# The window mask of a local attention layer: written into PSUM by VectorE instead of by two TensorE products, with the value projection moved ahead of the scores

## What is computed

```python
q, k, v = split(shift_tokens(x) @ Wqkv)            # 16 heads of 64
q = rotary(l2norm(q) * qs);  k = rotary(l2norm(k) * ksc)
# windows of 32 queries, each against its own 32 keys and the 32 before them
mask = (it < jb) | (it > jb + w) | (jb == -1)
sim = einsum('bhwie,bhwje->bhwij', bq, bk2) * 8.0
sim = where(mask, -finfo.max, sim)
out = einsum('bhwij,bhwje->bhwie', softmax(sim), bv2)
x = out @ Wo + x
```

## Time and profile before

| | us |
|---|---|
| median of 3 runs | 2062.97 (2062.51 to 2063.5) |
| the profiled execution | 2057.26 |
| its span in the profile | 2055.5 |
| PE busy | 1935.8 (94%) |
| DVE busy | 1512.3 (74%) |
| ACT busy | 1299.4 (63%) |
| POOL busy | 1012.4 (49%) |

### The profile page before, as it was taken

How to read it: one execution, slowest core, us unless ns; L and a number is a source line. 1 busy time by engine, 2 the same in 40 slices (tenths; PEclk the granted TensorE clock), 3 DMA queues, 4 the chain that set the end, 5 groups by cost and what they waited for, 6 DMA issues and landing times.

```text
span 2055.5 us, 46953 instructions
## 1 busy us (share of the span) xinstructions
PE 1935.8 (94%) x19084; PEld 1159.1 (56%) x19084; DVE 1512.3 (74%) x1720; ACT 1299.4 (63%) x1840; POOL 1012.4 (49%) x727
## 2 busy tenths in 40 slices
PE   6798887899999999999999999999999999999996
PEld 3121134466666666666666666666666666666662
DVE  4898355687777777787778777877787778777862
ACT  3387834566666666666667666766676667666752
POOL 6200133575556555555555555555555555555530
PEclk9799999899999999999999999999999999999998
DMA  4231010343434443344434434443354334443430
GB/s 126 46 75 29 8 39 9 104 132 101 108 88 113 124 128 90 98 103 129 122 96 112 104 101 122 123 104 91 101 139 119 95 88 112 114 110 83 117 93 16
DMA packets 105541, 195.87 MB, mean 95 GB/s; under 512 B 14288, under 2 KB 34256, under 8 KB 105072
## 3 DMA queue, kind: packets, MB, share of 16 engines
q1 hardware_dynamic: 105328, 192.88, 36.2%
HBM read 124.81 MB, written 54.79 MB: 87 GB/s over the span
## 4 chain that ended last, share of the span: by engine, by line
PE 78%; ACT 2%; issue 1%; POOL 1%; DVE 0%; DMA 0%; SPq 0%; ACTq 0%; POOLq 0%
PE ps L1392 16%; PE ps L1467 9%; PE ps L1422 9%; PE ps L1444 8%; PE ps L1401 8%; PE ps L1477 8%; PE ps L1496 6%; PE ps L1455 4%; PE ps L1432 4%; PE ps L1506 3%; PE ps L1417 2%; ACT l_v_tok L1558 1%; PE ps L1484 1%; POOL l_rot L1365 0%; POOL l_rot L1368 0%
## 5 line engine op out<-in xcount | busy, mean ns | idle before, releaser
L1365 POOL TENSOR_TENSOR l_rot<-l_rot,l_rot_s 128x1024 f32<-128x1024 f32 x192 | 455.1, 2371 | 1.0 <-DVE l_rot_s L1709 1.0
L1354 POOL COPY l_kb<-l_kb 128x512 f32<-128x512 f32 x95 | 63.1, 664 | 683.5 <-ACT l_kb L1592 683.5
L1368 POOL TENSOR_TENSOR l_rot<-l_rot,l_norms 128x1024 f32<-128x1024 f32 x192 | 365.1, 1902 | 15.0
L1697 DVE TENSOR_TENSOR l_rot<-ps,l_tab_c 128x1024 f32<-128x1024 f32 x192 | 234.9, 1224 | 165.5 <-ACT l_sq L1566 165.5
L1566 ACT ACTIVATE l_sq<-ps 128x1024 f32<-128x1024 f32 x192 | 196.8, 1025 | 206.5 <-PE ps L1392 204.0
L1709 DVE TENSOR_TENSOR l_rot_s<-ps,l_tab_s 128x512 f32<-128x512 f32 x384 | 245.6, 682 | 0.0
L1688 DVE TENSOR_REDUCE l_norms<-l_sq 128x16 f32<-128x1024 f32 x192 | 232.1, 1209 | 0.0
L1392 PE MATMUL ps<-l_wqkv,xsT 128*128 128x512 f32 x384 | 187.1, 611 | 16.9 <-ACT l_v_tok L1558 14.4
L1592 ACT ACTIVATE l_kb<-ps 64x1024 f32<-64x1024 f32 x192 | 195.7, 1019 | 1.3
L1575 ACT ACTIVATE l_norms<-l_norms 128x16 f32<-128x16 f32 x192 | 41.6, 217 | 233.0 <-POOL l_norms L1362 233.0
L1444 PE MATMUL ps<-l_vb,l_pT 128*32 128x128 f32 x6144 | 186.9, 273 | 1.6 <-ACT l_pT L1558 1.4
(11 more groups left out here) (171 smaller groups left out, 3132.3 us busy)
## 6 DMA issues: line engine op xcount, KB each, us to landing
l_vb<-v_scratch SPq DMA_DIRECT2D x336, 256.0 KB, 4.5
v_scratch<-l_v_tok SPq DMA_DIRECT2D x96, 512.0 KB, 4.8
l_vb<-v_scratch SPq DMA_DIRECT2D x48, 192.0 KB, 3.2
xsT<-xT SPq DMA_DIRECT2D x48, 135.8 KB, 2.5
l_xf<-xT SPq DMA_DIRECT2D x48, 128.0 KB, 2.3
stack<-scratch SPq DMA_DIRECT2D x72, 64.0 KB
l_wqkv_odd<-wqkv SPq DMA_DIRECT2D x9, 512.0 KB, 6.7
scratch<-parts SPq DMA_DIRECT2D x12, 256.0 KB, 2.8
```

The source lines that it names most:

```text
L1365: nc.gpsimd.tensor_tensor(rot[:, t % 2, n], rot[:, t % 2, n], rot_s[:, n], ALU.add).then_inc(added, 1)
L1368: nc.gpsimd.tensor_tensor(rot[:, t % 2, n], rot[:, t % 2, n], norms[:, t % 2, n, :, None].broadcast_to([P, HEADS, DH]), ALU.mult).then_inc ...
L1697: nc.vector.tensor_tensor(rot[:, t % 2, 1 - r], slot(name, t).rearrange("p n (h d) -> p (n h) d", d=DH), tab_c[:, 1 - r, t % TILES, None, ...
```

## The change

- `scores` loses its two mask products. A new VectorE function `lay_mask(t-1)` copies the fp32 mask of the tile's kind from the constants into the slot of the scores, 128 x 1024 elements, and counts `mask_laid`. It waits until the transposed k, which stood in that slot, has been copied out. It stands on VectorE between the sine part of k (in the hidden step: the scaled feed-forward input) and the cosine part of q. TensorE's scores wait for `mask_laid` in place of the transposed k's release.
- The transposes of q and k set `start` only on the first of the four in a bank, where `nc.tensor.transpose` set it on each.
- `project_v(t)` moves ahead of `scores(t-1)` on TensorE, and its turn in slot 1 stays behind the mean.
- `copy_v(t)` on ScalarE moves from behind `inverse_norm(t, 1)` to directly behind `inverse_norm(t, 0)`.
- The constants hold one [128, 2 x 64] fp32 mask in place of the [128, 512] one and the selection matrix; the two casts at the start of the layers go away.

```diff
-        mask = sb("l_mask", [P, BANK], BF16)
-        mask_sel = sb("l_mask_sel", [P, 2, P], BF16)
+        mask = const("wmask").rearrange("p (a k) -> p a k", a=2)
...
+            if has(t):
+                plan(("v", t), 1)
             if has(t - 1):
                 plan(("s", t - 1), 3)
             if has(t - 2):
                 plan(("o", t - 2), 0)
-            if has(t):
-                plan(("v", t), 1)
...
-                        m = nc.tensor.transpose(dst[:, c // 4, (c % 4) * P:(c % 4 + 1) * P],
-                                                rot[:, t % 2, "qk".index(name), 2 * c:2 * c + 2, :], ident)
+                        m = nc.tensor.matmul(dst[:, c // 4, (c % 4) * P:(c % 4 + 1) * P],
+                                             rot[:, t % 2, "qk".index(name), 2 * c:2 * c + 2, :], ident,
+                                             is_transpose=True, start=(c % 4 == 0), stop=True, skip_group_check=True)
...
                     wait_free(pe, "qT", t)
-                    wait_free(pe, "kT", t)
+                    wait(pe, mask_laid, t + 1)
                     wait(pe, carried, t)
-                    if t == 0:
-                        pe.wait_ge(consts_set, 3)
                     take(pe, "s", t)
                     dst = slot("s", t)
-                    opening = int(t % TILES == 0)
-                    for n in range(2):
-                        rows = slice(64 * n, 64 * n + 64)
-                        nc.tensor.matmul(dst[:, n, :], mask_sel[rows, opening, :], mask[rows, :], start=True, stop=False,
-                                         skip_group_check=True)
...
+                    if has(t):
+                        project_v(t)
                     if has(t - 1):
                         scores(t - 1)
                     if has(t - 2):
                         values(t - 2)
-                    if has(t):
-                        project_v(t)
...
                     if has(t):
                         inverse_norm(t, 0)
+                        copy_v(t)
...
                     if has(t):
                         inverse_norm(t, 1)
-                    if has(t):
-                        copy_v(t)
...
-                nc.vector.tensor_copy(mask[:, :], const("wmask")).then_inc(consts_set, 1)
-                nc.vector.tensor_copy(mask_sel[:, :, :], const("wsel").rearrange("p (a q) -> p a q", a=2))\
-                    .then_inc(consts_set, 1)
...
+                def lay_mask(t):
+
+                    wait_free(dve, "kT", t)
+                    nc.vector.tensor_copy(slot("s", t).rearrange("p n (h k) -> p (n h) k", k=2 * WINDOW),
+                                          mask[:, int(t % TILES == 0), None, :].broadcast_to([P, HEADS, 2 * WINDOW]))\
+                        .then_inc(mask_laid, 1)
+
...
                         nc.vector.tensor_tensor(xg[:, :], cen[:, :], rstd[:, :], ALU.mult).then_inc(xn_ready, 1)
+                    if has(t - 1):
+                        lay_mask(t - 1)
                     if has(t):
                         cosine_part(t, 1)
                         sum_squares(t, 1)
```

More of the change, by code:

```diff
@@ L44 @@
                   ("kmask", HEADS), ("vmask", GROUPS * HEADS), ("ropeC", 2 * TILES * DH),
-                  ("ropeS", 2 * TILES * DH), ("wmask", 8 * 2 * WINDOW), ("wsel", 2 * P)):
+                  ("ropeS", 2 * TILES * DH), ("wmask", 2 * 2 * WINDOW)):
     CONST[_name] = (_at, _n)
@@ L1148, in layers @@
         slot_free = [sem(f"l_slot{i}_free") for i in range(4)]
+        mask_laid = sem("l_mask_laid")
         maxed, exped, sum_ready, inv_ready = (sem("l_" + n) for n in ("maxed", "exped", "sum_ready", "inv_ready"))
@@ L1573, in inverse_norm @@
                     if part == 0:
-                        act.wait_ge(consts_set, 3)
+                        act.wait_ge(consts_set, 1)
                     nc.scalar.activation(norms[:, t % 2, 1 - r], norms[:, t % 2, 1 - r], ACT.Ln, scale=65536.0)\
@@ L1850, in shape_constants @@
         put(name, a.reshape(2, TILES, P, DH).transpose(2, 0, 1, 3))
-    m = np.zeros((P, 8, 2 * WINDOW))
+    m = np.zeros((P, 2, 2 * WINDOW))
     key = np.arange(2 * WINDOW)
-    for r in range(WINDOW):
+    for q in range(P):
+        r = q % WINDOW
         bad = (key < r) | (key > r + WINDOW)
-        m[r] = np.where(bad, -1e30, 0.0)
-        m[WINDOW + r] = np.where(bad | (key < WINDOW), -1e30, 0.0)
-    m[2 * WINDOW:] = m[:2 * WINDOW]
+        m[q, 0] = np.where(bad, -1e30, 0.0)
+        m[q, 1] = np.where(bad | ((key < WINDOW) & (q < WINDOW)), -1e30, 0.0)
     put("wmask", m)
[L1860 to L1865, removed]
     return c
```

## The result

The changed kernel takes 2128.87 us (median of 4 runs, 2125.66 to 2142.47) against 2062.74 us before: a ratio of 1.0306, 95% interval 1.0265 to 1.0348. It is 66 us slower; the forecast was 59 us slower, 2122 us, with a range of 2084 to 2155.

The account below looks back on a forecast made before the run. TensorE's own work was taken to bound the kernel. Norm-step cycles +32, clock loss +30, early steps -4 and drain +1 made +59 us on 2063, so 2122 us; range 2084 to 2155.

Parts of the forecast that it names:

- What bounds the kernel: Layers: TensorE's own instructions set the time almost throughout; work removed there saves its length, a wait added costs its length.
- The gain forecast for the last step: Last of the four successive steps: 15.05 us, that is -0.58, as small waits go with the mask products.
- The mask copy: VectorE, every step: 1.2 us, ending near k+7.9 in former idle time, hidden because TensorE reaches the scores at k+8.8.
- The lower value, 0.85 us: Mask copy on VectorE: some 0.85 us for 1024 elements, from the 512-element cast; the sum would be some 10 us smaller.
- the hold-up to 2.3 us: Rival: the mask copy is held up like the second cast, to 2.3 us; 2182 us in all, chance 0.05.
- The norm step: v waits in slot 1 for the centring, TensorE idle 3.1 us; 17.26 us against 15.08, +2.18.
- The hidden step: The second feed-forward product waits some 0.5 us for slot 3, freed near k+14.7: 18.1 us, +0.1.
- The clock: Behind the norm step's idle time TensorE's clock halves, three times in four, costing 1.7 us each: +30 us.
- The early steps: Steps 1 to 5: k's wait for v's copy goes, VectorE sets a pace near 13.7 us; -0.6 each, -4 in all.
- The rival without the clock loss: Norm step: the same idle time but the clock is held, +29, 2092 us; chance 0.18.
- The rival in which v isn't held: Norm step: the centring frees the slot before TensorE gets there, step 14.19 us; 2020 us in all, chance 0.08.
- Break-even: Norm step: without a clock loss the change costs nothing if the centring ends near k+9.4; each microsecond earlier gives back one.

Follow-up runs that it names:

- the mask copy alone: The change without its new order, v and its copy where they were before: 2125.95 us, ratio 1.0322 to the kernel before.
- the experiment with the other bank first: The change, but in the norm step v's product for slot 1's second bank goes ahead of the wait for the centring: 2095.75 us, ratio 1.0139.
- the new order alone: The kernel before with the change's order of v and its copy, the mask still by two TensorE products: 2140.96 us, ratio 1.0376.
- the experiment with other work in the idle time: The change plus three unused 128x512 products between mean and v in each norm step: 2100.8 us, ratio 1.0186 to the kernel before.
- the norm step in its old order: The change, but in the norm step v goes behind scores and values again, its copy behind q's inverse norm: 2036.13 us, ratio 0.987.

## Why the prediction was right

**What bounds the kernel.** Right. In the output step TensorE is busy 19.34 of 19.34 us, and 0.32 us came off exactly as the mask products went. Last step 15.08 us against 15.05 worked out. Counting what every step does once, in the step without waits, and adding each step's own piece and its wait gave all four step lengths within 0.15 us. The gain forecast for the last step, 0.58 us, was too large all the same: it was taken from the one last step in the earlier trace rows, which took 15.63 us, while the median before was 15.47. Measured are 0.39.

**The mask copy.** Right in size, 1226 ns for 1.2 us, and in place. The lower value, 0.85 us from the cast of 512 elements, is excluded, and so is the hold-up to 2.3 us: the 96 copies of the program took 1217 to 1229 ns, 95 of them with GpSimd busy for over 97% of their length. What had held up the second cast in the earlier trace rows may be read from the trace before: it ran until 359.59, and a GpSimd product that had begun ahead of it until 359.44. By the Trainium skill's page "VectorE: DVE Perf Modes", section "Why PSUM operands drop a tier", an fp32 instruction of VectorE with an operand in PSUM goes no faster than the plain rate. The trace agrees: the copy takes as long as VectorE's products of 1024 elements that read PSUM, 1.22 to 1.23 us. That v covers the copy was the forecast's other half; the mask copy alone showed what it costs without v in front, 0.7 to 1.0 us a step.

**The norm step.** Right: 17.26 us forecast without a clock loss, 17.36 measured; wait 3.1 us forecast, 2.90 measured from the end of the mean's record, and 3.06 from k+7.79, where a product of v could start in the experiment with the other bank first. The centring ended at k+10.80 for k+10.82.

**The hidden step.** Forecast 18.1 us with a wait of 0.5 us for slot 3, measured 17.97. The wait is there but shorter, about 0.3 us: the second feed-forward product starts at k+14.46 and the subtraction that frees the slot ends at k+14.32, where k+14.7 was forecast. So the step was forecast 0.1 us longer than before and came out 0.05 shorter.

**The clock.** Right in kind and size: three in four at 1.7 us made 1.3 a step, measured were 18 in 22 at 1.62, also 1.3 a step. One statement held only in part: the granted clock was to be low just behind the wait. In the 18 cases the drop began between 0.24 us before the restart and 1.43 us after it; in the step shown it was 0.98 for 1.4 us and fell then, into the scores.

**The early steps.** Mis-sized, and what sets their pace was wrong. Forecast -4 us, measured -1.7 from the first k projection to the first output projection (98.37 us against 100.04). VectorE's load was to set a pace of 13.7 us. The transposes of q and k follow each other every 13.9 us instead, where they did every 14.3 before, so a step gives 0.3 to 0.4 us and not 0.6. The first gives nothing: from the first k projection to the first transposes are 17.43 us, before 17.42. One distance in each kernel holds a clock loss and is longer, 15.51 us after and 15.32 before. With the new order alone the pace is the same 13.9 us, so it comes with the order. The chain of waits there runs through GpSimd (POOL in order of time):

```profile
404.22 0.61 POOL L1354 COPY l_kb<-l_kb 128x512 f32<-128x512 f32 x1 [5.88 <-ACT l_kb L1586]
...
409.51 2.36 POOL L1365 TENSOR_TENSOR l_rot<-l_rot,l_rot_s 128x1024 f32<-128x1024 f32 x1
411.95 1.90 POOL L1368 TENSOR_TENSOR l_rot<-l_rot,l_norms 128x1024 f32<-128x1024 f32 x1
418.12 0.61 POOL L1354 COPY l_kb<-l_kb 128x512 f32<-128x512 f32 x1 [4.26 <-ACT l_kb L1586]
```

It is a loop. GpSimd works on k and q from 404.22 to 413.85. Then TensorE transposes them and ScalarE copies the result, and only at 418.12, 13.90 us after its last such start, GpSimd can begin with the next tile. ScalarE's copy of v, which now stands ahead of the inverse norm of q, does not hold this up: that norm ends at 410.14, and GpSimd's rotation (L1365), which stands ahead of the product with it (L1368), only at 411.87.

**Sum.** +32 for the steps, +30 for the clock, -4 and +1 made +59. Measured by the medians, four steps without clock losses make +1.5 us (-0.32, +2.28, -0.05 and -0.39) where +1.4 was forecast, so 23 times that is +35. The clock makes 18 times 1.62, +29. The early steps make -1.7, and in the drain the last scores wait 2.09 us for the copy where they had waited 1.11 before, the +1 of the forecast. That is +63 of the 65.5 us in the trace; the rest is in single steps that were longer. So the measured 66 us lie 7 above the forecast by small terms, the early steps and the steps' lengths. The two large ones, the wait and the clock, came out as forecast.

The rival without the clock loss is what the experiment with other work in the idle time measures: 2101 us for the 2092 given, and in the layers +29.0 us for +29. The rival in which v isn't held is what the norm step in its old order approaches, 2036 us for the 2020 given. Break-even was put at a centring that ends near k+9.4, with each microsecond giving one back in each norm step. At k+8.7 this makes 23 times 0.7, 16 us faster; measured were 18.

## What to carry to other kernels

When work is moved ahead to cover a wait, look up what the moved piece itself waits for: here v took a PSUM slot behind the mean, and the scores and values that had stood between the two were the time in which the mean was consumed. Check this for the rare step too, not only for the common one; one step in four gave up more than the other three gained. Two edits that lose 60 us or more each alone can be a gain together once one bad place is mended (2031 to 2046 us here, against 2061 to 2064 before), so a change of this kind should be judged in parts. VectorE writes the mask where TensorE's products are then added, and the mask isn't 0. The Trainium skill's page "PSUM — Partial Sum Buffer", section "The four PSUM rules", calls 0 the only seed that is safe whatever the state of the bank's bits, which tell TensorE whether to add or to overwrite. No run here tried the transposes' flags by themselves.

## What the runs showed of the hardware that was not expected

The share of idle times after which TensorE's clock is halved differs with their length, at otherwise the same place of the program. Of 22 in one execution of each kernel: 0.32 us, none; 0.78 us, none; 2.04 us, 8; 2.82 us, 14; 2.90 us, 18. The last two are too close to be told apart by such counts. A loss costs 1.6 to 1.7 us in most cases; with the order alone it was 1.4 to 1.7, and once 2.9. The halved clock can begin as late as 1.4 us after the work has been taken up again in the changed kernel, so the slow records may stand one or two pieces behind the wait that caused them.
